# One gathered tile of 64 fetched row by row by SyncE and ScalarE, in a four-part graph network

## What is computed

```
x = layernorm(x + gated messages, summed per destination, then a GRU cell and a batch norm)
x = layernorm(x + 3 attention layers)       # k[src], v[src], softmax per destination
x = layernorm(x + 3 mean-aggregation layers)
x = layernorm(x + message layer)            # h[src] * an MLP of the edge features, summed

attention, one layer:  logits = sum(q[dst] * k[src]) / sqrt(128)
                       alpha  = softmax of logits over the edges of one dst
                       out    = segment_sum(alpha * v[src], dst) + skip,  relu between layers
```

## Time and profile before

| | |
|---|---|
| median of three executions | 7192.41 us (7189.78 to 7192.6) |
| the profiled execution | 7204.17 us |
| its span, first to last instruction | 7202.4 us |
| mean granted TensorE clock | 0.851 |
| busy: TensorE, VectorE, ScalarE, GpSimd | 77%, 65%, 31%, 69% |
| indirect DMAs of GpSimd in the attention layers, in the message layer | 2496, 832 |

### The profile page before, as it was taken

How to read it: one execution, slowest core, us unless ns; L and a number is a source line. 1 busy time by engine, 2 the same in 40 slices (tenths; PEclk the granted TensorE clock), 3 DMA queues, 4 the chain that set the end, 5 groups by cost and what they waited for, 6 DMA issues and landing times. The chain is left out here.

```text
span 7202.4 us, 119566 instructions
## 1 busy us (share of the span) xinstructions
PE 5539.1 (77%) x30345; PEld 4155.7 (58%) x30345; DVE 4713.5 (65%) x20339; ACT 2266.8 (31%) x5973; POOL 4979.1 (69%) x5179
## 2 busy tenths in 40 slices
PE   5675667777777767777777777789899997888886
PEld 4442344566566556666656556666666665666665
DVE  7985668466666556666636666664645546888887
ACT  1044442211114411113411111543333333454544
POOL 5777765577777577777577777647576674777774
PEclk6687888778888878888878888899999998989899
DMA  9433352577777567777557777667576662222222
GB/s 305 137 79 87 79 113 53 152 204 207 207 208 217 157 189 210 207 207 220 175 174 208 209 206 208 195 179 209 165 210 192 206 205 83 56 56 56 57 56 53
DMA packets 911842, 1151.30 MB, mean 160 GB/s; under 512 B 143281, under 2 KB 676465, under 8 KB 911249
## 3 DMA queue, kind: packets, MB, share of 16 engines
q1 hardware_dynamic: 689440, 673.54, 30.9%
q0 software_dynamic: 202464, 461.07, 23.8%
q10 hardware_dynamic: 19346, 9.66, 0.5%
HBM read 882.09 MB, written 261.74 MB: 159 GB/s over the span
## 5 line engine op out<-in xcount | busy, mean ns | idle before, releaser
L500 POOL DMA_INDIRECT G<-table_kv,idx x2496 | 2383.6, 955 | 964.4 <-issue 750.1
L1715 DVE SCALAR_TENSOR_TENSOR sums<-ramp,place,bank 128x128 f32<-128x128 f32 x2496 | 718.7, 344 | 1188.9 <-PE bank L1632 1104.7
L1622 PE MATMUL bank<-ident,G 128*128 128x128 f32 x2496 | 648.8, 338 | 698.7 <-DMA G<-table_kv,idx 691.9
L2149 POOL DMA_INDIRECT G<-table_h,src_idx x864 | 830.1, 961 | 465.5 <-issue 252.7
L1601 ACT COPY slab<-bank 128x512 f32<-128x512 f32 x624 | 364.8, 585 | 2298.6 <-PE bank L1622 2294.7
L500 POOL DMA_INDIRECT G<-table_h,idx x832 | 831.6, 1000 | 302.0 <-issue 229.2
L1632 PE MATMUL bank<-qT,slab 128*128 x4992 | 915.6, 341 | 100.9 <-issue 81.7
L1632 PEld LDWEIGHTS bank<-qT,slab 128*128 128x128 f32 x4992 | 800.7, 243 | 200.7 <-issue 199.0
L1622 PEld LDWEIGHTS bank<-ident,G 128*128 128x128 f32 x2496 | 384.1, 165 | 918.3 <-DMA G<-table_kv,idx 871.8
L1846 DVE TENSOR_SCALAR OH<-ramp,place,weight 128x128 f32<-128x128 f32 x2076 | 722.4, 357 | 16.0 <-issue 9.4
L2133 PE MATMUL bank<-sums,qT 128*128 128x418 bf16 (+1 forms) x3528 | 676.4, 334 | 38.6 <-DVEq L2209 14.1
(11 more groups left out here) (355 smaller groups left out, 9582.4 us busy)
## 6 DMA issues: line engine op xcount, KB each, us to landing
stash<-G SPq DMA_DIRECT2D x312, 512.0 KB
sums<-stash SPq DMA_DIRECT2D x624, 256.0 KB
sums<-adjacency SPq DMA_DIRECT2D x294, 522.5 KB
adjacency<-same SPq DMA_DIRECT2D x49, 1184.0 KB
same<-adjacency SPq DMA_DIRECT2D x90, 522.5 KB
G<-table_kv,idx POOLq DMA_INDIRECT x2496
sums<-adjacency SPq DMA_DIRECT2D x48, 408.0 KB
table_kv<-G SPq DMA_DIRECT2D x72, 256.0 KB, 2.9
```

Source lines behind the costliest of these rows:

```text
L500: pool.indirect_dma_start(G[:, s, 0:width], None, tab, bass.IndirectOffsetOnAxis(ap=idx[:, s:s + 1], axis=0)).then_inc(c_gather[s].sem, 16)
L1622: ins = pe.transpose(bank[q % 2][:, (s % QUAD) * P:(s % QUAD + 1) * P], G[:, s, 0:D], ident[:])
L1715: ins = dve.scalar_tensor_tensor(scratch[:, s, :], ramp[:], place[:, n * QUAD + s:n * QUAD + s + 1], bank[2 + q % 2][:, s * P:(s + 1) * P] ...
L2149: pool.indirect_dma_start(G[:, s, 0:D], None, table[l], bass.IndirectOffsetOnAxis(ap=src_idx[:, DENSE + t:DENSE + t + 1], axis=0)).then_in ...
```

## The change

One tile of every 64, slot 15 of every fourth turn (`FAR_TURNS = 4`, 13 tiles a layer), isn't gathered by GpSimd. Its 128 rows are fetched one at a time to a side buffer `far_rows`, each by a DMA of its own whose source address is a register, and when all are there one DMA copies the buffer to `G[:, 15]`.

* The source numbers of such a tile come as a line of 512 bytes (`far_src`, `sp_far_line`), and SyncE or ScalarE reads them from there into registers, up to eight at a time.
* Attention: the rows are spread over the eight halves before the tile's turn. After the store of each half SyncE issues 12 row DMAs, and ScalarE issues 2 after each quad's source numbers (4 a half). At the start of a layer, before the first store, SyncE issues 24 and ScalarE 8. Before the store of the first half of every fourth turn, SyncE waits until all rows and the store before have landed, and copies the tile to `G`.
* Message layer: SyncE alone issues 8 rows after each of its four loads of a turn, and the copy at the end of every fourth turn.
* SyncE's loops over turns in the attention layers are written out.

The core of the diff:

```diff
+FAR_TURNS = 4
+FAR_TILES = TURNS // FAR_TURNS
+FAR_SLOT = SLOTS - 1
+FAR_PARTS = 2 * FAR_TURNS
+FAR_ROWS = P // FAR_PARTS
+FAR_ACT = 2
+FAR_SP = FAR_ROWS - 2 * FAR_ACT
...
+        def far_nodes(kind, m, k, n):
+            _, nodes = nc.values_load_multi_w_load_instructions(
+                far_src[0:1, m % 2, k:k + n], engines=(kind,), min_val=0, max_val=NODES - 1,
...
+        def sp_far_rows(l, tab, width, m, k, n):
+            for at in range(k, k + n, 8):
+                some = min(8, k + n - at)
+                for r, node in enumerate(far_nodes(SP, m, at, some)):
+                    sp.dma_start(far_rows[at + r:at + r + 1, m % 2, 0:width], tab[bass.ds(node, 1), :]).then_inc(far_in[l][m % 2].sem, 16)
...
+        def gather_but_far(tab, width, stashed=False):
+            with pool.Fori(0, FAR_TILES) as m:
+                for u in range(FAR_TURNS):
...
+                            if s != FAR_SLOT or not is_far(u):
+                                pool.indirect_dma_start(G[:, s, 0:width], None, tab,
...
             def store(t, h):
-                sp.wait_ge(c_turned.sem, c_turned.turn(t, QUADS, 2 * h + 2))
-                sp.sem_inc(c_sp_issue.sem, 1)
+                if h == 0 and is_far(t):
+                    far_tile(t)
+                sp.wait_ge(c_turned.sem, c_turned.at(QUADS * t + 2 * h + 2))
...
+                far_rows_after(t, h)
...
+            def far_tile(t):
+                m = t // FAR_TURNS
+                sp.wait_ge(far_in[l][m % 2].sem, far_in[l][m % 2].at(16 * FAR_SP * FAR_PARTS * (m // 2 + 1)))
+                sp.wait_ge(far_in_act[m % 2].sem, far_in_act[m % 2].at(16 * 2 * FAR_ACT * FAR_PARTS * (m // 2 + 1)))
+                sp.wait_ge(c_stored[1].sem, c_stored[1].at(16 * t))
+                sp.dma_start(G[:, FAR_SLOT, :], far_rows[:, m % 2, :]).then_inc(far_landed.sem, 16)
...
+            sp_far_line(0)
+            far_rows_after(-1, 0)
+            far_rows_after(-1, 1)
...
         def act_attention(skip_bias):
+            for q in range(QUADS):
+                act_far_rows(-1, q)
...
                     quad_idx(t, q, c_turned)
+                    act_far_rows(t, q)
...
                 def turn(i, last):
                     for h in range(2):
...
+                        far_part(i, 2 * h)
                         if not last:
                             sp.wait_ge(c_h1.sem, c_h1.turn(i, 2, h + 1))
                             features(h, (i * 2 + (h + 2)) * PAIR)
+                        far_part(i, 2 * h + 1)
+                    if is_far(i):
+                        far_tile(i)
```

More of the change, by code:

```diff
@@ L326, in build_program @@
         c_tp = signal("tp_psum")
+        far_src_in = signal("far_src_in")
+        far_landed = signal("far_tile_landed")
+        far_in = [[signal(f"far_rows_in{l}_{k}") for k in range(2)] for l in range(TRANSFORMERS + 1)]
+        far_in_act = [signal(f"far_rows_in_act{k}") for k in range(2)]
+        far_read = signal("far_src_read")
         c_far = signal("distance")
@@ L555, in quad_loaded, with is_far, wait_landed @@
                 pe.wait_ge(c_loaded[s // QUAD].sem, c_loaded[s // QUAD].turn(i, 16, 16))
+        def is_far(t):
+            return t % FAR_TURNS == FAR_TURNS - 1
+        def wait_landed(engine, t, s):
+            far = (t + 1) // FAR_TURNS
+            if s != FAR_SLOT:
+                engine.wait_ge(c_gather[s].sem, c_gather[s].at(16 * (t + 1)))
+            elif is_far(t):
+                engine.wait_ge(far_landed.sem, far_landed.at(16 * far))
+            else:
+                engine.wait_ge(c_gather[s].sem, c_gather[s].at(16 * (t + 1 - far)))
@@ L1565, in load @@
+                sp.wait_ge(c_rows.sem, c_rows.at(QUADS * t + q + 1 - QUADS))
                 part = q % 2 * QUAD * D
                 sp.dma_start(v_rows[:, q * QUAD:(q + 1) * QUAD, :].rearrange("p s d -> p (s d)"),
[L1567 to L1572 removed]
@@ L1573, in sp_attention, with far_rows_after @@
-            with sp.Fori(0, EVEN_TURNS) as i:
+                             stash[t * 2 + q // 2:t * 2 + q // 2 + 1, :, part:part + QUAD * D].rearrange("a p d -> (a p) d")).then_inc(c_loaded[q].sem, 16)
+            def far_rows_after(t, h):
+                m, part = far_part_at(t, h)
+                if m is None:
+                    return
+                if part == 0:
+                    sp.wait_ge(far_src_in.sem, far_src_in.at(16 * (m + 1)))
+                    if m >= 2:
+                        sp.wait_ge(far_landed.sem, far_landed.at(16 * (m - 1)))
+                if part == 2 and m + 1 < FAR_TILES:
+                    if m:
+                        sp.wait_ge(far_read.sem, far_read.at(m))
+                    sp_far_line(m + 1)
+                sp_far_rows(l, table_kv, 2 * D, m, part * FAR_ROWS, FAR_SP)
@@ L1574, in sp_attention @@
+            sp_far_line(0)
+            far_rows_after(-1, 0)
+            far_rows_after(-1, 1)
+            for t in range(LAG - 1):
+                store(t, 0)
+                store(t, 1)
+            for t in range(EVEN_TURNS):
                 for q in range(QUADS):
                     if q % 2:
-                        store(i + (LAG - 1), q // 2)
-                    load(i, q)
+                        store(t + LAG - 1, q // 2)
+                    load(t, q)
             stores = [(QUADS * t + 2 * h + 1, 0, t, h) for t in range(EVEN_TURNS + LAG - 1, TURNS) for h in range(2)]
@@ L1584, in sp_attention, with act_far_rows @@
                     store(t, part)
+        def act_far_rows(t, q):
+            m, part = far_part_at(t, q // 2)
+            if m is None:
+                return
+            if part == 0 and q == 0:
+                act.wait_ge(far_src_in.sem, far_src_in.at(16 * (m + 1)))
+                if m >= 2:
+                    act.wait_ge(far_landed.sem, far_landed.at(16 * (m - 1)))
+            k = part * FAR_ROWS + FAR_SP + q % 2 * FAR_ACT
+            for r, node in enumerate(far_nodes(mybir.EngineType.Activation, m, k, FAR_ACT)):
+                act.dma_start(far_rows[k + r:k + r + 1, m % 2, :], table_kv[bass.ds(node, 1), :]).then_inc(far_in_act[m % 2].sem, 16)
+            if part == FAR_PARTS - 1 and q % 2:
+                act.sem_inc(far_read.sem, 1)
         def act_attention(skip_bias):
+            for q in range(QUADS):
+                act_far_rows(-1, q)
             for n in range(ALL_SLOTS):
@@ L1962, in build_program @@
             loop_passed()
+            far_passed()
             for c in c_stored + c_loaded:
```

74 lines of the change are left out of this document (49 added, 25 removed).

## The result

The changed kernel takes 7252.11 us (median, 7244.79 to 7270.86), the kernel before in the same runs 7192.51 us: ratio 1.0091, 95% interval [1.0079, 1.0103], 65 us slower. The forecast was 7169, 24 us faster, its range 7145 to 7245. The profiled execution took 7254.16 us, its span is 7252.4, where the earlier trace rows belong to one of 7202.4.

A forecast was written before the change was run, and what follows sets the result against it. GpSimd's issuing was taken to bound all gather stages. Removed gathers -65.8 us, layer starts +22 and far turns +20 gave -24 us: 7180 us profiled, 7169 us median; range 7145 to 7245 us.

The forecast's parts named there:

- What bounds the kernel now: All four gather stages: bound by GpSimd's issuing, 1.25 us a gather in attention, 1.305 in the message layer.
- What the change removes: 13 gathers a layer: 48.8 us in attention and 17.0 us in the message layer, together 65.8 us.
- The price of a row: SyncE's time for one fetched row, register work and gaps included: taken as 0.50 us, bounds 0.43 and 0.68.
- Loading the source numbers: SyncE's load of up to eight source numbers into registers: 0.276 us, with its gap 0.33 us.
- SyncE in a half turn of attention: SyncE's store, register loads, twelve rows and v loads end at 8.0 us; GpSimd needs 10.0, so 2 us to spare.
- Far turns: Attention, halves before a far tile's copy: late stores charged 0.5 us for each of 39 turns, 20 us, bounds 0 to 58.
- Start of a layer: Attention: line, 24 rows and register loads ahead of the first store delay GpSimd 8.7, 13.6 and 0 us, together 22 us.
- ScalarE: nothing in the steady part: Attention: ScalarE's two rows and one register load a quad, 1.3 us, cost nothing in the steady part.
- Message layer, SyncE 96% occupied and fits: Four message turns and a far tile take SyncE 78.5 us, GpSimd 82.2; SyncE keeps up, so the 17 us stay.
- (c): Rival: row price as forecast, but far turns in attention cost 1.5 us each; 7207 us, chance 0.15.
- (b): Rival: rows cost 0.56 us, so only the message layer becomes bound by SyncE; 7238 us, chance 0.12.
- GpSimd waiting on stores in nearly every half: A sign named for the forecast being wrong; if right, total store waits would rise from 46 to 80 or 90 us.

The follow-up runs named there:

- e3: The whole change with the far tiles left out: no gathers, row fetches or copy for them; 7135.62 us, ratio 0.9936 to the kernel before.
- e1: The change in the message layer alone, attention layers gathering as in the kernel before; 7164.67 us, ratio 0.9978 to the kernel before.
- e9: The whole change, but SyncE loads a half's source numbers into registers ahead of the store's wait, not behind the store; 7198.71 us, ratio 1.0019.
- e11: The whole change without SyncE's rows and register loads in the attention layers; 7169.33 us, ratio 0.9974 to the kernel before.
- e14: The whole change with SyncE and ScalarE fetching eight rows each a half, and the far tile's copy behind the store; 7172.20 us, ratio 0.9962.
- e13: The whole change, but GpSimd gathers the first far tile of each attention layer; 7247.96 us, ratio 1.0069 to the kernel before.
- e10: The whole change without ScalarE's rows and register loads in the attention layers; 7243.14 us, ratio 1.0075 to the kernel before.
- e12: The whole change with ScalarE fetching four rows a quad instead of two, SyncE eight a half instead of twelve; 7161.02 us, ratio 0.9966.
- e5: The whole change with SyncE's register loads ahead of the store's wait, on a chip where the kernel before took 9636 us; ratio 1.0415.

## Why the prediction was wrong, step by step

Two steps failed above all: the price of a register load, 0.33 us for what took 1.60 behind a store, and "SyncE keeps up with 2 us to spare", which took the average of halves that aren't alike. All steps in turn:

* **What bounds the kernel now.** Right: GpSimd's pace of 1.25 us stayed, and no gather was slowed.
* **What the change removes, 65.8 us.** Mis-sized: e3 measured 46 (35 to 57). The 17.0 of the message layer hold (e1: 16 us). The 48.8 of attention don't: in a far turn GpSimd comes sooner to a store that doesn't come sooner.
* **The price of a row, 0.50.** It came out at 0.41, below my lower bound of 0.43. The sixteen-partition loads at 0.31 us were not a floor for a DMA of one row. The rule that a one-partition copy leaves extra work to the sequencer (the Trainium skill, DMA: Bandwidth & Descriptors, "Why a DMA increments its semaphore by 16 and not by 1") was my reason to fear 0.68. By that rule the traces agree on what happens: the semaphore of 672 row DMAs has 1336 updates, two a row, and a row moves as one packet of 1024 bytes. No cost of it shows in 0.228 us on SyncE. ScalarE's first row of a quad takes 0.46 and the following ones 0.23.
* **Loading the source numbers, 0.33 each.** This is the term that failed first. I read 0.276 from ten loads in the adjacency stage, and charged it behind a store, where it took 1.60. Two loads and their gaps are 2.2 us of a half, not 0.66. Together with the cheaper rows (12 x 0.09) that makes a half 0.5 us longer than forecast, and as measured 1.0 (9.0 us from the store to the end of the second v load, the median of 91 halves in which SyncE waited for less than 0.6 us, not 8.0). Of the 89 us between forecast and result the change of place in e9 gives 48 back, though not by SyncE's time alone.

  The Trainium skill (DMA: Bandwidth & Descriptors, "Latency and other measured facts") gives a tensor_load a floor of about 600 ns, and I set it aside. By that rule, the traces agree in part: 0.72 in the message layer and 0.56 behind a row are near it. It isn't a floor here: the ten loads of the earlier trace rows take 0.264 at least, and e9 shows 0.30 for the second of two in a row. The 1.60 behind a store is far over it. I should have kept that figure as one of the bounds.
* **SyncE in a half turn of attention: "keeps up with 2 us to spare".** Wrong, and the second step that failed. The sum of issue times, 8.0 of 10.0 us, left out that the second v load waits for TensorE's sums. The trace of before had it: SyncE's waits of the v loads for those sums are its largest in attention, 1615.6 us, and around 2000 us its stores stand 10.1 to 11.9 us apart in most halves and 8.3 to 8.8 in the others. The forecast's 8.0 us would just have fitted into the short ones; the 9.0 that it became don't. In the trace of the change around 2000 us the second v load goes out 9.9 to 11.4 us after the store in about every second half; in the others, in which all is ready, it ends 8.6 to 9.5 us after the store, with hardly a pause, and the next store is late. In order, an engine with a wait in the middle has not its average slack but what the shorter interval leaves. The forecast also took the landing of a store as given; right behind both v loads it took 5.0 us and not 4.0.
* **Far turns, 20 us.** I thought the stores late only there. They are late there too, and dearer than 0.5 us each: the 36 first halves of far turns (the last of each layer gates nothing) stall for 53.5 us instead of 7.2, 1.3 us more each. All other halves have the other 56 of the 102 us. Of the 46, e3 has 23 that come with the missing gather alone; the rest is the copy's by the traces of e11 (56.2) and e14 (17.0), and by the times open.
* **Start of a layer, 22 us.** Right in the trace, 21.4 us. In the time e13 shows 12, with three gathers given back and not clear of noise.
* **ScalarE: nothing in the steady part.** Right: e10, e12.
* **Message layer, SyncE 96% occupied and fits.** Right (it waits for VectorE for 89 of 1062 us), by errors that partly cancel: rows 0.09 us cheaper (128 of them in four turns, -11.5), register loads 0.44 dearer (16, +7).
* **Rivals.** (c) has the far turns' price about right, 1.3 for 1.5 us, and ends at 7207 for want of the rest. (b) came within 14 us of the result, by luck: it had SyncE bound in the message layer, by dearer rows. None had a register load behind a store, or a v load's wait in the middle of the half. What I had named as a sign of being wrong, "GpSimd waiting on stores in nearly every half", didn't come either: 68 waits instead of 60, and longer ones, 121.0 us together where I had said 80 or 90.

## What to carry to other kernels

Before giving an in-order engine more work, list its waits and not only its busy time: the slack is that of the shortest interval between two things that others wait for, with the waits in between left standing. What is loaded into registers from memory belongs ahead of the wait, not behind a large transfer of the same queue; that change of place was about 50 us here. A store that others wait for landed later in these traces where large loads went out right ahead of it (5.0 us, not 4.0), so look at what stands directly in front of it too. And a saved instruction on the bound engine pays its full pace only where that engine doesn't come to a wait sooner: leave the work out altogether once, to know what there is to win.

## What the runs showed of the hardware

* A load of register values from on-chip memory by SyncE took 0.56 us behind a row DMA, 0.72 in the message layer, 1.60 behind the DMA of a 512 KB store, and 0.30 right behind another such load (medians). When it no longer stood behind the store (e9), the third row DMA there took 0.68 instead of 0.23 us. That both wait for the same thing in the queue is my reading; no run isolates it.
* A 512 KB store landed 5.0 us after the end of its issue (median) where both v loads of 256 KB had been issued in the 1.3 us ahead of it, and 4.0 where the first was over 3 us ahead, in the same kernel.
* A DMA of one 1 KB row costs SyncE 0.228 us, less than the sixteen-partition loads of the earlier trace rows (0.31 at least, 0.43 in the median); with its register work a row starts every 0.41 us.
* Two of five groups of runs met a chip on which the same kernel took a third longer, with bursts in which SyncE's instructions stood 0.7 to 1.4 us apart (e5). The chip of the first such group was at the usual time in a later one. Ratios from there (1.0415 for a kernel that is 1.0019 elsewhere) don't carry over.
